# Two tiles of the first normalised rows moved to ScalarE, and rows of x, stores and two additions placed elsewhere in their queues, in a float32 linear-attention block on one core

## The chip, the core and the metric

The kernel runs on one core of a Trainium2 chip. The engines of the core work side by side and meet only at semaphores: TensorE (PE in the profile; PEld is its weight load), VectorE (DVE), ScalarE (ACT), GpSimd (POOL) and SyncE (SP), which here only issues transfers. The metric is the device time of one execution in microseconds, lower is better; the time of a kernel is the median of several executions.

## The reference

```python
x  = hidden_states                      # 4 sequences x 512 tokens x 512, float32
xn = layernorm(x)
qkv = silu(xn @ w_qkv.T)                # 16 heads of 128: q, k, v
for each block of 64 tokens:            # decayed linear attention
    out   = (q * q_decay) @ kv + ((q @ k.T) * diag_decay) @ v
    kv    = block_decay * kv + (k * k_decay).T @ v
out = norm_w * out * rsqrt(mean(out^2) + eps)
s   = (sigmoid(xn @ w_gate.T) * out) @ w_out.T
scores = softmax(xn @ router_w.T + router_bias)        # 64 experts, top 8
f   = xn * sum(top_w) + top_w @ expert_bias[top_idx]
return x + s * silu(f)
```

## The kernel before, in words

Every float32 product is made of three: each operand is split into a part that TensorE takes exactly (`_hi`, rounded by ScalarE) and a rest (`_lo`, the difference, from GpSimd for weights and from VectorE for tokens), and hi x hi, hi x lo and lo x hi are summed in PSUM.

The four sequences are worked in two halves of two sequences (`bp` 0 and 1), each half in eight steps, one for a pair of heads: steps `ss` 0 to 15. A step has four weight groups, QK0, VAL, QK1 and GATE. From step 1 on each group is computed with seven block products (`p1` ... `p7`) over blocks of the transposed tokens, of which four are sums of others (`T1` to `T4`) in Strassen's manner; VectorE's `e1` ... `e7` join the products, and ScalarE applies the activations. Step 0 uses plain products (`direct_block`).

The order on each engine is written out by hand, one function per engine; each engine runs its list from top to bottom, and a wait holds everything behind it.

Opening. SP loads four row tiles of the first sequence (128 tokens x 512 each, into `acc`), the constants, the first weight group (`land_a`), the four tiles of the second sequence, and later the sequences of the second half. VectorE computes statistics of the first four tiles and a Newton step of 1/sqrt (`row_stats`, `row_roots`), then normalises tiles 0, 1 and 2; ScalarE normalises tile 3 (`normalise`, L975), between the two halves of the first weight split (`direct_hi(0, 0)`, `direct_hi(0, 1)`, L1005). GpSimd makes the rests of these weights (`direct_lo`, L1420). PE transposes the tiles strip by strip (`fill(0, 0)` to `fill(0, 3)`, L491; `rows_there` holds the waits on the tiles), ScalarE and VectorE take each result (`take_fill`, L994 and L1634), and `direct_block(0)` begins (L524 to L526).

Transition between the halves. The transposed tokens of the second half wait in device memory. In step 7 SP loads them block by block (`load_block`, L373 and L374; four transfers of 256 KB for each block) into the places that the step's GATE products have left free, in the order B21, T2, T1, T3, T4, B22, after it has issued the load of step 8's VAL weights (L316, 512 KB). In step 8 (`close`) the first half is finished: for each of eight row tiles `sum0` (VectorE, L1824) joins the experts' product with the row of x from `res_buf` (`load_res`, L426), ScalarE applies Silu, `scale0` (L1837) multiplies, `finish0` (GpSimd, L1483) adds the row of x, and `store0` (L430) writes the tile out. The ring `res_row` holds four rows, so `load_res(t + 4)` comes after `finish0(t)`. Rows 4 and 5 are loaded ahead of the load of the next QK0 weights and the turning of the keys (`swap_keys`), rows 6 and 7 behind them. The last two additions, `finish0(6)` and `finish0(7)`, and their stores belong to step 9: on GpSimd they stand ahead of the work on the QK1 weights (`raw_lo`, `weight_sums`, `sums_lo`), on SP ahead of the load of the GATE weights (L323), which waits until `sums_lo` has freed `land_a`.

In every step from 1 on the values are turned through device memory: `values_out` (L354) writes a block of 256 KB, `values_back` (L361) reads two of them back in four transfers of 128 KB made of short packets, once for each sequence, and `kv_products` (L677) on PE waits for them.

Of the kernel before, what the change touches and what calls it, by code (L numbers as in the profile page):

```python
# [15 lines left out]
NCH = SEQ // CH  # L16
# [4 lines left out]
TILES = 2 * NCH  # L21
# [16 lines left out]
def lightning_block(nc: bass.Bass, x, wgrp, wv, wo, consts_d, router_w, expert_b, out):  # L38
# [9 lines left out]
    with ExitStack() as ctx:  # L48
# [262 lines left out]
        def _(sp):  # L311
# [58 lines left out]
            def load_block(blk):  # L370
                at = place(PAIRS, blk)
                for k in range(2):
                    sp.dma_start(xt_hi[:, at, k, :].bitcast(F32), spill_hi[2 * blk + k]).then_inc(block_in[blk], 16)  # L373
                    sp.dma_start(xt_lo[:, at, k, :].bitcast(F32), spill_lo[2 * blk + k]).then_inc(block_in[blk], 16)  # L374

            def step(pair, ss):
                close = ss == PAIRS
                after = (pair + 1) % PAIRS
                if close:
                    sp.wait_ge(top_turned, 2)  # L380
                    for t in range(4):
                        load_res(t)
                swap_keys(ss, 0)
                if ss == PAIRS - 1:

                    sp.wait_ge(router_made, 2)
                    load_block(B11)
                values_out(ss, 0)
                if ss == PAIRS + 1:
                    store0(6)  # L390
                    store0(7)
                load_group(pair, ss, GATE)
                load_out(pair, ss)
                values_out(ss, 1)
                values_out(ss, 2)
                values_back(ss, 0)
                values_out(ss, 3)
                values_back(ss, 1)
                if close:
                    for t in range(2):  # L400
                        store0(t)
                        load_res(t + 4)
                if ss < LAST:
                    load_group(after, ss + 1, QK0)
                swap_keys(ss, 1)
                if ss == LAST:
                    return
                if close:
                    for t in range(2, 4):
                        store0(t)  # L410
                        load_res(t + 4)
                load_group(after, ss + 1, VAL)
                if ss == PAIRS + 1:
                    load_block(B12)
                if ss == PAIRS - 1:
                    for blk, used in ((B21, P2), (T2, P6), (T1, P5), (T3, P7), (T4, P4), (B22, P3)):
                        sp.wait_ge(prod, prods(group(ss, GATE)) + used)
                        load_block(blk)
                if close:
                    store0(4)  # L420
                load_group(after, ss + 1, QK1)
                if close:
                    store0(5)
# [50 lines left out]
        def _(pe):  # L474
# [18 lines left out]

            def rows_there(bp, b, c):

                if bp == 0 and c < 3 - b:
                    pe.wait_ge(ln_row, 3 * b + c + 1)
                elif bp == 0:
                    pe.wait_ge(ln_row_a, c if b else 1)
                elif b == 0:  # L500
                    pe.wait_ge(ln_row, 5 + c + 1)
                else:
                    pe.wait_ge(ln_row_a, 3 + c + 1)

            def direct_block(j, quarters=range(4)):

# [456 lines left out]
        def _(act):  # L963
# [291 lines left out]
            act.wait_ge(eps_set, 2)  # L1255
            act.preload_act_table(ACT.Sqrt)
            root_std(0)
            direct_hi(0, 0)
            normalise(0, 0, 0, 3)
            direct_hi(0, 1)  # L1260
            for f in range(4):
                take_fill(0, f)
            values_hi()
            root_std(1)
# [114 lines left out]
        def _(pool):  # L1379
# [5 lines left out]

            def token_sums0():

                pool.wait_ge(ln_row, 5)
                pool.wait_ge(ln_row_a, 3)
                pool.wait_ge(xt_turned, filled(0, 1))  # L1390
                pool.tensor_tensor(half_rows(0, 0), half_rows(1, 0), half_rows(0, 0), ALU.subtract).then_inc(t_row, 1)
                pool.wait_ge(t_row, 1)
                pool.wait_ge(xt_turned, filled(0, 5))
                pool.tensor_tensor(half_rows(1, 0), half_rows(1, 1), half_rows(1, 0), ALU.subtract).then_inc(t_row, 1)
                pool.wait_ge(t_row, 2)
                pool.wait_ge(xt_turned, filled(0, 7))
                pool.tensor_tensor(half_rows(1, 1), half_rows(1, 1), half_rows(0, 0), ALU.subtract).then_inc(t_row, 1)
                pool.wait_ge(t_row, 3)
                pool.tensor_tensor(half_rows(0, 1), half_rows(0, 1), half_rows(1, 1), ALU.subtract).then_inc(t_row, 1)

            def token_sum1(i):
# [3 lines left out]
                dst = half_rows(*((0, 0), (1, 0), (1, 1), (0, 1))[i])  # L1405
                first, second = ((b12, b11), (b22, b12), (b22, half_rows(0, 0)), (b21, half_rows(1, 1)))[i]
                if i == 0:
                    pool.wait_ge(ln_row, 5 + NCH)
                    pool.wait_ge(ln_row_a, 3 + NCH)
                pool.wait_ge(xt_turned, filled(0, 9 + 2 * i))  # L1410
                pool.wait_ge(t_row, NCH + i)
                pool.tensor_tensor(dst, first, second, ALU.subtract).then_inc(t_row, 1)
# [79 lines left out]
            def step(bp, ss):  # L1492
# [10 lines left out]
                add_square(bp0, before, 1, 0)  # L1503
                sums_lo(ss, VAL)
                add_square(bp0, before, 1, 1)
                if ss == PAIRS + 1:
                    finish0(6)
                    finish0(7)
                raw_lo(ss, QK1)
                weight_sums(ss, QK1)  # L1510
                sums_lo(ss, QK1)
                if ss == LAST:
                    direct_lo(FINAL, 0)
                    direct_lo(FINAL, 1)
# [58 lines left out]
        def _(dve):  # L1573
# [403 lines left out]
            row_stats(0, range(NCH))  # L1977
            row_roots(0)
            dve.wait_ge(ln_stat, LN_DONE[1])
            for c in range(3):  # L1980
                normalise(0, 0, c)
            for f in range(4):
                take_fill(0, f)
# [158 lines left out]
```

## Time and profile before

| | |
|---|---|
| median of 3 runs | 1076.3 us (1075.11 to 1077.16) |
| profiled execution, own time | 1073.37 us |
| profiled execution, span of its instructions | 1071.6 us |
| PE busy | 1047.8 us, 98% of the span |
| PE weight load busy | 894.9 us, 84% |
| VectorE, ScalarE, GpSimd busy | 752.5, 514.8, 634.3 us |
| chain that ended last | PE 88%, DVE 4%, DMA 3%, SP's queue 2%, POOL 2% |

The span is that of one profiled execution; its own time is 1.8 us longer, and the median of the runs lies 2.9 us above that. Busy time of PE is modelled from pipelined matmuls. The chain is followed back from the last instruction to what released each piece of work.

### The profile page before, as it was taken

Reading aid. Unit: us, or ns where it says so; the run is one execution under the profiler, and the core shown is the slowest. Engines: PE = TensorE matmul, PEld = TensorE weight load, DVE = VectorE, ACT = ScalarE, POOL = GpSimd, SP = SyncE. Lnnn points to the kernel's source line nnn. Section 1 sums busy time; section 2 is a strip of 40 time slices with the busy share of each in tenths; the row PEclk is TensorE's granted clock in tenths of the full one; section 3 lists DMA queues with packets and bytes.
Section 4 is the critical chain, followed back from the end, with each engine's and each line's share of the span. In section 5 each row is a group of like instructions: output and inputs, shape, how many; then the busy total and the mean of one; then the engine's idle time right before and its main releaser. Section 6 shows DMA issues by size and latency. Waiting matters only on the chain.

```text
span 1071.6 us, 15997 instructions
## 1 busy us (share of the span) xinstructions
PE 1047.8 (98%) x5626; PEld 894.9 (84%) x5626; DVE 752.5 (70%) x1287; ACT 514.8 (48%) x806; POOL 634.3 (59%) x513
## 2 busy tenths in 40 slices
PE   5999999999999999999999999999999999999997
PEld 5898888888888888888888788888888888888886
DVE  6857667676765768767677776756767766876866
ACT  4845353453536335453554535445453543535345
POOL 3837475565747557474746856657474755747435
PEclk9999999999999999999999999999999999999999
DMA  7173524435252442526856255352525335252442
GB/s 242 65 279 100 130 79 129 108 98 118 54 134 69 128 89 72 136 68 168 271 191 155 96 141 141 103 114 60 143 70 133 90 101 107 59 123 85 130 127 80
DMA packets 259920, 128.12 MB, mean 120 GB/s; under 512 B 223360, under 2 KB 223488, under 8 KB 259840
## 3 DMA queue, kind: packets, MB, share of 16 engines
q1 hardware_dynamic: 259840, 127.09, 43.7%
q8 instruction: 46, 0.75, 0.3%
q14 instruction: 34, 0.28, 0.1%
HBM read 86.95 MB, written 40.11 MB: 119 GB/s over the span
## 4 chain that ended last, share of the span: by engine, by line
PE 88%; DVE 4%; DMA 3%; SPq 2%; POOL 2%; issue 2%; ACT 1%; POOLq 0%; DVEq 0%
PE st_ps L536 17%; PE st_ps L538 16%; PE st_ps L537 16%; PE out_ps L711 5%; PE score_ps L658 5%; PE out_ps L713 5%; PE out_ps L712 5%; PE head_ps L694 5%; PE head_ps L697 4%; PE tk_ps L677 4%; PE st_ps L524 1%; PE st_ps L525 1%; PE st_ps L526 1%; DMA xt_lo<-spill_lo 1%; DMA k_squares<-v_t 1%
## 5 line engine op out<-in xcount | busy, mean ns | idle before, releaser
L536 PE MATMUL st_ps<-xt_hi,w_hi 128*128 128x512 f32 x826 | 336.8, 408 | 2.6 <-DVE gated L1677 1.6
L538 PE MATMUL st_ps<-xt_hi,w_lo 128*128 128x512 f32 x826 | 323.2, 391 | 0.0
L537 PE MATMUL st_ps<-xt_lo,w_hi 128*128 128x512 f32 x826 | 322.1, 390 | 0.0
L1446 POOL TENSOR_TENSOR w_lo<-land_a,w_hi 128x1024 fp32r<-128x1024 f32 x44 | 107.8, 2449 | 130.0 <-ACT w_hi L1040 130.0
L538 PEld LDWEIGHTS st_ps<-xt_hi,w_lo 128*128 128x128 f32 x826 | 155.0, 188 | 34.6
L536 PEld LDWEIGHTS st_ps<-xt_hi,w_hi 128*128 128x128 f32 x826 | 155.6, 188 | 32.1 <-DVE gated L1677 1.8
L537 PEld LDWEIGHTS st_ps<-xt_lo,w_hi 128*128 128x128 f32 x826 | 155.7, 189 | 27.9
L1426 POOL TENSOR_TENSOR w_lo<-land_a,w_hi 128x768 fp32r<-128x768 f32 x44 | 84.2, 1913 | 147.1 <-ACT w_hi L1035 147.1
L711 PE MATMUL out_ps<-wo_hi,gate_hi 128*128 128x512 f32 x240 | 96.2, 401 | 0.8 <-DVE acc L1762 0.6
L1764 DVE TENSOR_TENSOR acc<-acc,out_ps 128x512 f32<-128x512 f32 x104 | 71.2, 685 | 32.2 <-PE out_ps L713 31.0
L713 PE MATMUL out_ps<-wo_hi,gate_lo 128*128 128x512 f32 x240 | 93.7, 391 | 0.0
L712 PE MATMUL out_ps<-wo_lo,gate_hi 128*128 128x512 f32 x240 | 93.5, 390 | 0.0
L1477 POOL TENSOR_TENSOR acc_sq<-acc_sq,square 128x512 f32<-128x512 f32 x60 | 77.1, 1284 | 25.6 <-ACT square L1131 25.6
L694 PE MATMUL head_ps<-probs,v_row 128*128 128x128 f32 x496 | 85.6, 275 | 0.0
L694 PEld LDWEIGHTS head_ps<-probs,v_row 128*128 128x128 f32 x496 | 74.6, 191 | 5.4 <-issue 0.7
L1087 ACT ACTIVATE k_t<-k_t 128x512 f32<-128x512 f32 x30 | 19.0, 632 | 111.0 <-DVE k_t L1683 111.0
L697 PE MATMUL head_ps<-q_t,state 128*128 128x128 f32 x372 | 71.9, 275 | 0.0
L1749 DVE TENSOR_TENSOR gate_lo<-gated,gate_hi 128x512 fp32r<-128x512 f32 x60 | 70.5, 1177 | 0.5
L658 PEld LDWEIGHTS score_ps<-q_t,k_t 128*128 128x128 f32 x512 | 66.5, 191 | 4.6
L1745 DVE SCALAR_TENSOR_TENSOR gated<-gated,head_ps 128x512 f32<-128x512 f32 x62 | 42.5, 685 | 39.5 <-ACT gated L1081 18.6
L658 PE MATMUL score_ps<-q_t,k_t 128*128 128x128 f32 x512 | 67.3, 274 | 0.0
L1035 ACT ACTIVATE w_hi<-land_a 128x768 fp32r<-128x768 f32 x44 | 37.1, 844 | 58.4 <-DMA land_a<-wgrp_dram 45.2
(330 smaller groups left out, 2069.7 us busy)
## 6 DMA issues: line engine op xcount, KB each, us to landing
land_a<-wgrp_dram SPq DMA_DIRECT2D x48, 512.0 KB, 3.7
v_row<-v_squares SPq DMA_DIRECT2D x120, 128.0 KB, 3.2
k_row<-k_squares SPq DMA_DIRECT2D x120, 96.0 KB, 2.9
v_squares<-v_t SPq DMA_DIRECT2D x45, 256.0 KB, 2.6
land_b<-wo_dram SPq DMA_DIRECT2D x16, 512.0 KB, 4.6
land_b<-wgrp_dram SPq DMA_DIRECT2D x14, 512.0 KB, 4.2
k_squares<-state SPq DMA_DIRECT2D x15, 384.0 KB, 2.3
k_squares<-v_t SPq DMA_DIRECT2D x15, 384.0 KB, 4.7
```

The costliest lines, as they stand in the source:

```text
L536: pe.matmul(ps[:, :], w_h2, x_h2, start=first and k == 0, stop=False, skip_group_check=True)
L537: pe.matmul(ps[:, :], w_h2, x_l2, start=False, stop=False, skip_group_check=True)
L538: end = pe.matmul(ps[:, :], w_l2, x_h2, start=False, stop=last and k == 1, skip_group_check=True)
L658: last = pe.matmul(score_ps[:, at], k_t[:, b, at], q_t[:, h, b, at], start=True, stop=True)
L694: last = pe.matmul(ps[:, at], v_row[:, b, h, c, :], probs[:, b, c, :], start=True, stop=c == 0)
L697: last = pe.matmul(ps[:, at], state[:, b, c - 1, :], q_t[:, h, b, at], start=False, stop=True)
L711: pe.matmul(ps[:, :], hi[:, h, at], wo_hi[:, h, :], start=h == 0, stop=False)
L712: pe.matmul(ps[:, :], hi[:, h, at], wo_lo[:, h, :], start=False, stop=False)
L713: last = pe.matmul(ps[:, :], lo[:, h, at], wo_hi[:, h, :], start=False, stop=h == 1)
L1426: pool.tensor_tensor(flat(w_lo[:, n % 2, 0:3, :, :]), flat(landing(ss, g)[:, 0:3, :, :]), flat(w_hi[:, n % 2, 0:3, :, :]).bitcast(F32), AL ...
L1446: pool.tensor_tensor(flat(w_lo[:, n % 2, 3:7, :, :]), flat(landing(ss, g)), flat(w_hi[:, n % 2, 3:7, :, :]).bitcast(F32), ALU.subtract).th ...
L1477: pool.tensor_tensor(cols_b, cols_b, square[:, :], ALU.add).then_inc(sq_added, 1)
```

## The change

On ScalarE tiles 2 and 3 of the first sequence are normalised ahead of both halves of the first weight split, and the first `take_fill` comes between the halves; VectorE normalises only tiles 0 and 1. The counts that others wait for follow. In step 7 block B21 is loaded ahead of step 8's VAL weights. In step 8 tile 2 is stored and row 6 of x loaded with the first group, ahead of the next QK0 weights and the key turning. In step 9 `finish0(6)` and `finish0(7)` stand behind the QK1 weights on GpSimd, and their two stores behind `values_back(ss, 0)` on SP.

```diff
+            def renew_block(blk, used):
+                sp.wait_ge(prod, prods(group(PAIRS - 1, GATE)) + used)
+                load_block(blk)
...
                 values_out(ss, 0)
-                if ss == PAIRS + 1:
-                    store0(6)
-                    store0(7)
                 load_group(pair, ss, GATE)
                 load_out(pair, ss)
                 values_out(ss, 1)
                 values_out(ss, 2)
                 values_back(ss, 0)
+                if ss == PAIRS + 1:
+                    store0(6)
+                    store0(7)
                 values_out(ss, 3)
                 values_back(ss, 1)
                 if close:
-                    for t in range(2):
+                    for t in range(3):
                         store0(t)
                         load_res(t + 4)
...
                 if close:
-                    for t in range(2, 4):
-                        store0(t)
-                        load_res(t + 4)
+                    store0(3)
+                    load_res(7)
+                if ss == PAIRS - 1:
+                    renew_block(B21, P2)
                 load_group(after, ss + 1, VAL)
...
                 if ss == PAIRS - 1:
-                    for blk, used in ((B21, P2), (T2, P6), (T1, P5), (T3, P7), (T4, P4), (B22, P3)):
-                        sp.wait_ge(prod, prods(group(ss, GATE)) + used)
-                        load_block(blk)
+                    renew_block(T2, P6)
+                    renew_block(T1, P5)
+                    renew_block(T3, P7)
+                    renew_block(T4, P4)
+                    renew_block(B22, P3)
...
-                if bp == 0 and c < 3 - b:
-                    pe.wait_ge(ln_row, 3 * b + c + 1)
+                if bp == 0 and c < 2:
+                    pe.wait_ge(ln_row, 2 * b + c + 1)
                 elif bp == 0:
-                    pe.wait_ge(ln_row_a, c if b else 1)
+                    pe.wait_ge(ln_row_a, 2 * b + c - 1)
...
             root_std(0)
+            normalise(0, 0, 0, 2)
+            normalise(0, 0, 0, 3)
             direct_hi(0, 0)
-            normalise(0, 0, 0, 3)
+            take_fill(0, 0)
             direct_hi(0, 1)
-            for f in range(4):
+            for f in range(1, 4):
                 take_fill(0, f)
...
                 add_square(bp0, before, 1, 1)
+                raw_lo(ss, QK1)
+                weight_sums(ss, QK1)
+                sums_lo(ss, QK1)
                 if ss == PAIRS + 1:
                     finish0(6)
                     finish0(7)
-                raw_lo(ss, QK1)
-                weight_sums(ss, QK1)
-                sums_lo(ss, QK1)
...
-            for c in range(3):
+            for c in range(2):
                 normalise(0, 0, c)
```

## Rows read from the trace of the kernel before

**Rows 1.** Waits of PE: line, waited for whom, us in all, times, longest

```profile
PE out_ps L491 <- DVE acc L1623: 11.2, 2, 10.2
PE st_ps L536 <- DVE gated L1677: 1.6, 1, 1.6
...
PE st_ps L536 <- DMA xt_lo<-spill_lo: 0.8, 1, 0.8
```

**Rows 2.** Timeline of PE from 640 to 650 us

```profile
645.33 0.91 PE L677 MATMUL tk_ps<-v_row,k_row 128*128 128x128 f32 x6 [1.13 <-issue]
```

**Rows 3.** Busy us by window: length, PE, PEld, DVE, ACT, POOL, clock, DMA, GB/s

```profile
300.00:500.00 200.00, 200.00 (x1056) 170.58 (x1055) 143.30 (x252) 92.69 (x144) 118.59 (x97) 1.00 0.43 108
520.00:530.00 10.00, 10.00 (x59) 8.72 (x58) 7.96 (x12) 4.67 (x7) 5.96 (x4) 1.00 0.98 368
```

**Rows 4.** Timeline of the opening: start us, length us, engine, line, operation

```profile
9.51 2.47 DVE L1623 TENSOR_SCALAR acc<-acc,mean_var,rstd 128x512 f32<-128x512 f32 x3
9.73 0.63 ACT L1005 ACTIVATE w_hi<-land_a 128x512 fp32r<-128x512 f32 x1 [1.45 <-DMA land_a<-wgrp_dram]
...
10.27 0.80 ACT L975 ACTIVATE acc<-acc,ln_shift,rstd 128x512 f32<-128x512 f32 x1
10.44 2.67 POOL L1420 TENSOR_TENSOR w_lo<-land_a,w_hi 128x512 fp32r<-128x512 f32 x2 [9.57 <-ACT w_hi L1005]
...
12.77 0.60 ACT L994 ACTIVATE xt_hi<-out_ps 128x512 fp32r<-128x512 f32 x1 [1.18 <-PE out_ps L491]
...
15.96 0.69 DVE L1634 TENSOR_TENSOR xt_lo<-head_ps,xt_hi 128x512 fp32r<-128x512 f32 x1 [0.16 <-ACT xt_hi L994]
```

**Rows 5.** Tile acc from 9 to 13 us: durations in ns, smallest, median, largest

```profile
L1623 DVE TENSOR_SCALAR acc<-acc,mean_var,rstd x3: 540/545/1553, 9.5 to 10.4; 128x512 f32<-128x512 f32 x3
```

**Rows 6.** Chain that ended last, opening: start us, us, what

```profile
12.04 0.69 PE out_ps L491 x2
...
15.29 0.43 PE st_ps L524
...
16.10 0.23 PE st_ps L526
```

**Rows 7.** Tile land_b from 515 to 560 us, with its transfers' time to landing

```profile
L316 SPq DMA_DIRECT2D land_b<-wgrp_dram x1: 656/656/656, 518.1 to 518.1; - x1
L1035 ACT ACTIVATE w_hi<-land_b x1: 847/847/847, 527.5 to 527.5; 128x768 fp32r<-128x768 f32 x1
...
DMA to landing us min/median/max: 4.6/4.7/4.8
```

**Rows 8.** Timeline of POOL from 560 to 600 us

```profile
568.13 3.79 POOL L1483 TENSOR_TENSOR acc<-acc,res_row 128x512 f32<-128x512 f32 x3
```

**Rows 9.** Timeline of SP's queue around the seventh row of x

```profile
573.39 0.43 SPq L426 DMA_DIRECT2D res_row<-x_dram  x1
...
586.73 0.43 SPq L426 DMA_DIRECT2D res_row<-x_dram  x1
```

**Rows 10.** Timeline of DVE from 585 to 600 us

```profile
591.35 0.76 DVE L1824 SCALAR_TENSOR_TENSOR v_ps<-res_row,ffn_small,v_ps 128x512 f32<-128x512 f32 x1 [3.25 <-DMA res_row<-x_dram]
...
594.94 2.84 DVE L1749 TENSOR_TENSOR gate_lo<-gated,gate_hi 128x512 fp32r<-128x512 f32 x1
```

**Rows 11.** Timeline of POOL from 600 to 650 us

```profile
613.62 3.00 POOL L1483 TENSOR_TENSOR acc<-acc,res_row 128x512 f32<-128x512 f32 x2
```

**Rows 12.** Timeline of SP's queue in step 9

```profile
625.83 0.34 SPq L323 DMA_DIRECT2D land_a<-wgrp_dram  x1
...
627.18 1.56 SPq L354 DMA_DIRECT2D v_squares<-v_t  x2
633.88 3.03 SPq L361 DMA_DIRECT2D v_row<-v_squares  x4
...
639.78 3.20 SPq L361 DMA_DIRECT2D v_row<-v_squares  x4
```

**Rows 13.** Transfers issued from 636 to 645 us: count, KB each, us to landing

```profile
v_squares<-v_t SPq DMA_DIRECT2D x1, 256.0 KB, 2.8
```

More of the change, by code:

```diff
@@ L494, in rows_there @@
             def rows_there(bp, b, c):
-                if bp == 0 and c < 3 - b:
-                    pe.wait_ge(ln_row, 3 * b + c + 1)
+                if bp == 0 and c < 2:
+                    pe.wait_ge(ln_row, 2 * b + c + 1)
                 elif bp == 0:
-                    pe.wait_ge(ln_row_a, c if b else 1)
+                    pe.wait_ge(ln_row_a, 2 * b + c - 1)
                 elif b == 0:
-                    pe.wait_ge(ln_row, 5 + c + 1)
+                    pe.wait_ge(ln_row, NCH + c + 1)
                 else:
-                    pe.wait_ge(ln_row_a, 3 + c + 1)
+                    pe.wait_ge(ln_row_a, NCH + c + 1)
             def direct_block(j, quarters=range(4)):
@@ L1386, in token_sums0 @@
             def token_sums0():
-                pool.wait_ge(ln_row, 5)
-                pool.wait_ge(ln_row_a, 3)
+                pool.wait_ge(ln_row, NCH)
+                pool.wait_ge(ln_row_a, NCH)
                 pool.wait_ge(xt_turned, filled(0, 1))
@@ L1407, in token_sum1 @@
                 if i == 0:
-                    pool.wait_ge(ln_row, 5 + NCH)
-                    pool.wait_ge(ln_row_a, 3 + NCH)
+                    pool.wait_ge(ln_row, TILES)
+                    pool.wait_ge(ln_row_a, TILES)
                 pool.wait_ge(xt_turned, filled(0, 9 + 2 * i))
```

## The prediction, made blind

> **What bounds the kernel now.** I read five views: the waits of PE, busy time by window, the timeline and chain of the opening, the tile view of `land_b`, and the timelines of each engine around the transition (steps 7 to 9).
>
> The waits of PE come first. They name three places: the opening (11.2 us, of which 10.2 are the first wait and 1.0 a second one for a tile normalised by VectorE), and in the transition 1.6 us for VectorE's joining and 0.8 us for a block of spilled tokens [rows 1]. PE's timeline has a fourth, 1.13 us before `kv_products` of step 9, labelled "issue" [rows 2]. Elsewhere there is next to nothing: in a long window of the steady state PE is busy for all 200 of 200 us [rows 3]. There no edit on another engine can gain anything; only the stretches where PE waits can. The reader should see that the four parts of the change touch just these places. PE's waits are short and in a row, so what one gives back is kept only if the engines that feed PE come forward too.
>
> **The opening.** VectorE's three normalisations begin at 9.51 and take 2.47 us [rows 4]. The tile view shows why: two took 0.54 us, the third 1.55 us [rows 5], and that one ran while GpSimd made weight rests from 10.44 on [rows 4]. PE's third and fourth strip of `fill(0, 0)` start only at 12.04 and take 0.69 us, so to 12.73 [rows 6].
>
> After the change ScalarE starts its two tiles at about 9.5, when VectorE's own begin. At 0.80 us each [rows 4] both are done by 11.1. VectorE's two need 2 x 0.54 = 1.1 us and end at 10.6, and GpSimd can't be in their way, since it waits for `direct_hi(0, 0)`, now 11.1 to 11.75 (0.63 us). PE needs half of the 0.69 us after 11.1, with a tenth or so for the signal: 11.6, where it was 12.73. That is 1.1 us. The three fills behind it come 1.1 us earlier too, and `direct_block(0)` could start at 14.2, not 15.29 [rows 6].
>
> Do the others keep up? ScalarE: `take_fill(0, 0)` 11.75 to 12.35 (0.60 us) instead of from 12.77; `direct_hi(0, 1)` to 13.0; fills 1 and 2 to 14.2, fill 3 after PE's at 14.2, to 14.8. VectorE's rest of fill 3 then ends near 15.6, where it was 15.96 + 0.69 = 16.65 [rows 4]. The weights' first rest, now moved behind, is one of two in 2.67 us: 11.75 + 1.34 = 13.1, still ahead of 14.2. So the delayed weight split costs nothing; its cover is 1.1 us, and beyond that it would cost one for one. VectorE goes on from fill 3 to the second sequence's statistics, so the gain of 1.0 to 1.1 us is handed on along the chain. I take 1.0.
>
> The matmuls of the chain are spaced 0.43 us at 15.29 and 0.23 us from 16.10 [rows 6]: PE's rate at 1.2 and at 2.4 GHz for 512 columns. If the rise comes earlier with PE's work, all 1.0 stays. If it stays at 16.1, then 1.9 us of block products run at the low level instead of 0.8; the additional 1.1 us do half the work, and 0.55 us is lost. Bounds: 0.5 and 1.1. By the Trainium skill, "TensorE: Matmul & The Clock Gate", Part 1, recent activity releases the clock, and at a point that varies from run to run; that allows either case, and by its activity rule the sum would be 1.0, with a rise fixed in time 0.5. Whether the rise moves is not shown by this trace.
>
> **B21 ahead of VAL (step 7).** VAL's load was issued at 518.1 and landed 4.7 us later, at 522.8; ScalarE took it at 527.5, released by PE [rows 7]. Four issues of B21 come before it now, 1.8 us with the gaps between, and 1 MB, 2.8 us at 368 GB/s [rows 3]. The bytes decide: 525.6. Even both added whole, 527.4, just meets ScalarE. So no cost. Nor a gain: the wait that PE has here (0.8 us [rows 1]) is for a block that is issued later, and the bytes ahead of that one are the same. I take 0; bounds 0 and +0.8 (if the stall went away by a luckier order). If VAL came later than 527.5, ScalarE's whole list would be held, with the VectorE joins of the last GATE group behind it.
>
> **Row 6 earlier (step 8).** `finish0` of tiles 0, 1 and 2 starts at 568.13 and takes 3.79 us, to 571.9 [rows 8]. SP issued row 5 at 573.39 and would come to `store0(2)` at 573.8: nothing to wait for, and row 6 is issued at about 574.3 instead of 586.73 [rows 9]. VectorE waited 3.25 us, to 591.35, for that row alone (586.73 + 4.6) [rows 10]; with row 6 landed near 579 the wait is gone, and what is late next is PE's own product. PE saw 1.6 us of it [rows 1]. SP issues two transfers more (about 0.9 us) ahead of the QK0 weights and the key turning, in a gap of its queue. I take 1.5 for PE, since the `e4` that follows still trails PE by some 0.1 us. Lower bound: VectorE is held later by GpSimd, which ran a weight rest while `gate_lo` took 2.84 us [rows 10] and is not moved by this edit. If VectorE falls in with it again, its next joins stay where they were and PE waits for them instead. A third of the gain, 0.5 us, would be left; at worst 0. Upper bound 1.6.
>
> **finish0(6), (7) and their stores (step 9).** The two additions held GpSimd from 613.62 for 3.00 us [rows 11], in front of the QK1 weights. Behind those they delay nobody that I find; the QK1 rests end about 3 us earlier, and with them the GATE load of 625.83 (L323) that waits for them: about 622.8. It and the `wo` load, 1 MB together (2.8 us), then are out of the way when the value blocks are written at 627.18; before, the blocks were queued behind them, and SP could issue the first `values_back` only at 633.88 [rows 12]. Two issues end at 628.74, and a block lands in 2.8 us when nothing is ahead [rows 13]: 631.5 at the latest, 2.4 us earlier. From one `values_back` to the other it was 5.9 us [rows 12]; the stores now lie between, two issues of 0.45 us and 512 KB, 1.4 us at 368 GB/s. 631.5 + 5.9 + 1.4 = 638.8, or 1.0 us before the old 639.78. `kv_products` stood 1.13 us for this second swap [rows 2]. I take 1.0 for PE; upper bound 1.13; lower bound -1.4, if the first swap does not move and the stores only push the second.
>
> **The sum.** 1.0 + 0 + 1.5 + 1.0 = 3.5 us, from 1073.4 of the profiled execution to 1069.9. The runs' median is 2.9 above that execution; taking the same distance, 1076.3 - 3.5 = 1072.8.
>
> **Rivals.**
>
> *The clock rise stays.* For it: nothing in the trace ties it to the work. Against: it came after PE had been busy without a gap from 12.04 on [rows 6], so a PE that starts earlier may have it earlier. The opening gives 0.5: 1073.3. Chance 0.15.
>
> *GpSimd holds VectorE after row 6.* For: the 1.55 us normalisation [rows 5] and the 2.84 us `gate_lo` [rows 10] show how VectorE stands still beside GpSimd. Against: VectorE comes past that place over 1.6 us earlier, before GpSimd's long instruction. Row 6 gives 0.5: 1073.8. Chance 0.12.
>
> *The stores hold the last value swap.* The first swap doesn't move, and the stores push the second by 1.4: 1.0 + 1.5 - 1.4 = 1.1, so 1075.2. Chance 0.10.
>
> *The change does not do what it says.* The stalls are gone, but PE meets the next late engine some us further on and gets nothing from steps 8 and 9: only the opening, or 1075.8. PE's full 200 us window [rows 3] speaks against it for the steady state, the chain of close waits for it in the transition. Chance 0.08.
>
> *Slower.* The same two stores, but written at the rate of the short packets around them: a swap of 512 KB took from 639.78 to 645.33 [rows 2, 12], 5.6 us. If the first swap does not move, the second comes 5.6 us later, and PE's wait grows by that: 1.0 + 1.5 - 5.6 = -3.1, so 1079.4. It decides from the point where the second swap is issued over 2.5 us after 639.8. Against: writes of whole rows don't come in short packets. Chance 0.04.
>
> **How the numbers follow.** The forecast has 0.51. About 0.2%, 2.2 us, is what a measurement of this kernel can tell from no change, so faster means below 1074.1. The forecast and the first two rivals lie below (0.78 together, of which I count 0.06 as falling short, since the second is 0.3 us from the line): 0.72. Same: the third and fourth, and that 0.06: 0.24. Slower: 0.04. The range: at the low end all upper bounds, 1.1 + 0.8 + 1.6 + 1.1 = 4.6, or 1071.7, rounded to 1071.5; at the high end it takes in the third rival, 1075.3.
>
> **What the changed profile would show.** Opening: one strip wait less, PE's chain into `direct_block(0)` near 14.2; both VectorE normalisations at 0.54 us; GpSimd's first weight rest from about 11.8. If the third and fourth strip still start near 12, step one is wrong. The spacing of matmuls tells when the clock rises. Step 7: VAL still landed when ScalarE asks for it, the 0.8 us wait for the spilled block still there. Step 8: no wait for `res_row`, and no 1.6 us wait of PE at L536. Step 9: the first `values_back` over 2 us nearer to its `values_out`, no "issue" wait at L677. The prediction fails if PE's waits in the transition add up to over 2 us again under other names.

## The result, and the profile after

| | before | changed |
|---|---|---|
| median | 1075.92 us (4 runs, 1075.11 to 1077.16) | 1069.46 us (4 runs, 1068.64 to 1070.33) |
| profiled execution, own time / span | 1073.37 / 1071.6 us | 1068.64 / 1066.8 us |

The medians differ by 6.5 us. The ratio is 0.9948, 95% interval 0.9932 to 0.9964, which is 5.6 us, 3.9 to 7.3. The prediction had 3.5 us and 1072.8, and its range began at 1071.5. The direction was right, the size too small by this comparison, and the level outside the range. In a longer comparison, on one chip with more executions, the same code has 1070.3 against 1074.4 and the ratio 0.9966 (0.9952 to 0.9979), which is 3.7 us, 2.3 to 5.2 (e5 below), close to the forecast gain. The two profiled executions differ by 4.7.

PE's waits in the changed kernel (line, waited for whom, us in all, times, longest):

```profile
PE out_ps L499 <- DVE acc L1633: 9.8, 1, 9.8
PE out_ps L499 <- DVE xt_lo L1644: 1.3, 1, 1.3
PE st_ps L544 <- DMA xt_lo<-spill_lo: 1.3, 2, 0.8
PE out_ps L719 <- DVE acc L1772: 0.5, 1, 0.5
```

Of the waits of before [rows 1] the second one for a tile is gone from the first line, the one for `gated` is gone, and the "issue" wait [rows 2] is gone. The wait for the spilled blocks has grown from 0.8 to 1.3 us, in two pieces. PE's timeline has them:

```profile
534.07 0.47 PE L544 MATMUL st_ps<-xt_hi,w_hi 128*128 128x512 f32 x1 [0.44 <-DMA xt_lo<-spill_lo]
...
539.46 0.47 PE L544 MATMUL st_ps<-xt_hi,w_hi 128*128 128x512 f32 x1 [0.81 <-DMA xt_lo<-spill_lo]
```

How the gain builds up can be read from one recurring instruction, VectorE's first copy into `k_t` (twice in a step; L1677 before, L1687 after). Four of them in the changed kernel:

```profile
503.25 0.69 DVE L1687 COPY k_t<-st_ps 128x512 f32<-128x512 f32 x1 [1.15 <-PE st_ps L546]
...
571.96 0.69 DVE L1687 COPY k_t<-st_ps 128x512 f32<-128x512 f32 x1 [0.53 <-PE st_ps L546]
...
605.18 0.69 DVE L1687 COPY k_t<-st_ps 128x512 f32<-128x512 f32 x1 [2.08 <-PE st_ps L546]
...
667.40 0.69 DVE L1687 COPY k_t<-st_ps 128x512 f32<-128x512 f32 x1 [2.08 <-PE st_ps L546]
```

| copy in | before | changed | difference | added since the last |
|---|---|---|---|---|
| step 1 | 94.22 | 92.65 | -1.57 | -1.57 |
| step 7, second | 504.71 | 503.25 | -1.46 | +0.11 |
| step 8, second | 572.73 | 571.96 | -0.77 | +0.69 |
| step 9, first | 608.08 | 605.18 | -2.90 | -2.13 |
| step 10, first | 672.14 | 667.40 | -4.74 | -1.84 |
| step 15, second | 1019.46 | 1014.73 | -4.73 | 0.00 |

All of the change is made in the opening and in steps 8 and 9, and from step 10 on the difference stands still, as PE's full window [rows 3] had it.

**Opening.** Timeline of the changed kernel:

```profile
9.10 1.52 ACT L983 ACTIVATE acc<-acc,ln_shift,rstd 128x512 f32<-128x512 f32 x2 [1.24 <-DVE ln_shift L1627]
9.10 1.00 DVE L1633 TENSOR_SCALAR acc<-acc,mean_var,rstd 128x512 f32<-128x512 f32 x2
...
9.79 1.36 PE L499 MATMUL out_ps<-consts,acc 128*128 128x128 f32 x4 [9.79 <-DVE acc L1633]
...
10.53 0.61 ACT L1013 ACTIVATE w_hi<-land_a 128x512 fp32r<-128x512 f32 x1
...
11.22 2.51 POOL L1430 TENSOR_TENSOR w_lo<-land_a,w_hi 128x512 fp32r<-128x512 f32 x2 [10.36 <-ACT w_hi L1013]
...
14.38 0.69 DVE L1644 TENSOR_TENSOR xt_lo<-head_ps,xt_hi 128x512 fp32r<-128x512 f32 x1 [0.16 <-ACT xt_hi L1002]
```

ScalarE and VectorE start together at 9.10, each with two tiles; PE has all four strips in one run of 1.36 us; GpSimd starts only at 11.22, when VectorE is long done. The answers to [rows 4]: VectorE 1.00 for two instead of 2.47 for three, the rest of fill 3 at 14.38 instead of 15.96. The chain, against [rows 6]:

```profile
11.15 0.85 PE tk_ps L499 x4
...
13.71 0.43 PE st_ps L532
...
14.96 0.23 PE st_ps L532
```

The first block product is at 13.71, not 15.29, and the spacing falls from 0.43 to 0.23 us at 14.96, not 16.10: in these two executions the rise of the clock came 1.1 us earlier. That it went with the work is not shown: e5, the same kernel again, starts its block products 0.1 us before this one, and by PE's timeline its first spacing of 0.23 us comes only at 15.88 (15.94 in before, 14.79 to 15.03 in the changed kernel).

**B21 ahead of VAL.** The tile view of `land_b`, against [rows 7]:

```profile
L316 SPq DMA_DIRECT2D land_b<-wgrp_dram x1: 430/430/430, 518.8 to 518.8; - x1
L1043 ACT ACTIVATE w_hi<-land_b x1: 848/848/848, 526.0 to 526.0; 128x768 fp32r<-128x768 f32 x1
...
DMA to landing us min/median/max: 4.8/5.1/5.5
```

VAL is issued at 518.8 and lands 4.8 to 5.5 us later, by 524.3; ScalarE takes it at 526.0, released by PE. The order cost ScalarE nothing.

**Row 6.** SP's queue and VectorE, against [rows 9, 10]:

```profile
573.39 0.48 SPq L434 DMA_DIRECT2D res_row<-x_dram  x1
...
585.63 0.43 SPq L434 DMA_DIRECT2D res_row<-x_dram  x1
```

```profile
588.22 0.76 DVE L1834 SCALAR_TENSOR_TENSOR v_ps<-res_row,ffn_small,v_ps 128x512 f32<-128x512 f32 x1 [0.87 <-PE v_ps L755]
...
592.00 0.68 DVE L1759 TENSOR_TENSOR gate_lo<-gated,gate_hi 128x512 fp32r<-128x512 f32 x1
```

Row 6 is issued at 573.39 (586.73 before), row 7 at 585.63. VectorE's `sum0(6)` runs at 588.22 and waited 0.87 us for PE's own product, and `gate_lo` takes 0.68 us where it took 2.84.

**Step 9.** SP's queue and PE's value products, against [rows 2, 12]:

```profile
620.03 0.34 SPq L323 DMA_DIRECT2D land_a<-wgrp_dram  x1
...
623.80 1.88 SPq L354 DMA_DIRECT2D v_squares<-v_t  x2
627.46 3.23 SPq L361 DMA_DIRECT2D v_row<-v_squares  x4
630.74 1.15 SPq L438 DMA_DIRECT2D out_dram<-acc  x2
...
634.94 3.20 SPq L361 DMA_DIRECT2D v_row<-v_squares  x4
```

```profile
640.61 0.91 PE L685 MATMUL tk_ps<-v_row,k_row 128*128 128x128 f32 x6
```

The GATE load is issued at 620.03, the first value swap at 627.46, 3.7 us after its blocks were begun at 623.80 (6.7 before), and PE starts the second value products with no wait.

### The profile page after: what moved, and what is told of

Its sections match the earlier page's. It is cut to its first block, busy times and chain, and to the rows that moved or that the text cites. A ratio compares the mean times of both kernels' runs of the same rounds, so it can differ in the third digit from the quotient of the medians.

```text
span 1066.8 us, 15997 instructions
## 1 busy us (share of the span) xinstructions
PE 1047.1 (98%) x5626; PEld 895.0 (84%) x5626; DVE 750.0 (70%) x1286; ACT 515.5 (48%) x807; POOL 634.2 (59%) x513
## 4 chain that ended last, share of the span: by engine, by line
PE 92%; DVE 2%; DMA 1%; issue 1%; POOL 1%; ACT 1%; SPq 0%; POOLq 0%; DVEq 0%
PE st_ps L544 18%; PE st_ps L546 17%; PE st_ps L545 17%; PE score_ps L666 5%; PE out_ps L719 5%; PE out_ps L721 5%; PE out_ps L720 5%; PE head_ps L702 5%; PE tk_ps L685 4%; PE head_ps L705 4%; PE st_ps L532 1%; PE st_ps L534 1%; PE st_ps L533 1%; DMA xt_lo<-spill_lo 1%; POOL acc L1567 1%
## 5 line engine op out<-in xcount | busy, mean ns | idle before, releaser
L1436 POOL TENSOR_TENSOR w_lo<-land_a,w_hi 128x768 fp32r<-128x768 f32 x44 | 83.9, 1906 | 147.9 <-ACT w_hi L1043 147.9
L1759 DVE TENSOR_TENSOR gate_lo<-gated,gate_hi 128x512 fp32r<-128x512 f32 x60 | 66.4, 1109 | 0.5
```

Source lines behind the costliest of these rows:

```text
L1436: pool.tensor_tensor(flat(w_lo[:, n % 2, 0:3, :, :]), flat(landing(ss, g)[:, 0:3, :, :]), flat(w_hi[:, n % 2, 0:3, :, :]).bitcast(F32), AL ...
```

## The experiments

Each kernel is timed against before in five rounds on one chip; a difference in us is the ratio's, with its 95% interval. The runs of before had medians of 1074.72 (35 runs), 1074.42 (23) and 1074.51 (23) in the three comparisons.

**The parts alone.** e1 has only the opening:

```diff
             root_std(0)
+            normalise(0, 0, 0, 2)
+            normalise(0, 0, 0, 3)
             direct_hi(0, 0)
-            normalise(0, 0, 0, 3)
+            take_fill(0, 0)
             direct_hi(0, 1)
```

> The opening part alone. The trace of the changed kernel has step 1 earlier by 1.57 us, of which 0.4 is an earlier landing of the first rows of x. If the edit makes the gain and it is kept through the transition: 1.1 to 1.2 us faster, all seven steps before step 8 earlier by that much. If the wait for the spilled blocks in step 8 is set by the transfers and not by PE, 0.3 to 0.7 us of it is given back there: 0.5 to 0.9 us faster. If the opening holds what the profiled execution of before hides (the runs' median moved by 6.5 us, the profiles only by 4.7): 2.5 us or more.

Measured: 1073.19 us, ratio 0.9983 (0.9973 to 0.9994), 1.8 us faster (0.6 to 2.9). Its profile is 0.88 us ahead of the profile of before in step 1 and 0.84 to 0.90 ahead through step 9: nothing was given back in step 8. From step 10 on it is 1.55 us ahead and more, since PE waited 0.6 us at the value products of step 9 and not 1.1, although nothing there was changed. At its end only 0.2 us of this is left; where it goes is shown in the last part of this section.

e2 has only row 6 and the store of tile 2:

```diff
-                    for t in range(2):
+                    for t in range(3):
                         store0(t)
                         load_res(t + 4)
...
-                    for t in range(2, 4):
-                        store0(t)
-                        load_res(t + 4)
+                    store0(3)
+                    load_res(7)
```

> Row 6 of x and the store of tile 2 earlier in step 8, alone. By the two traces this part gave 2.1 us up to the first product of step 9 and 0.5 more in it: 2.1 to 2.6 us faster. By the prediction's step (the 1.6 us wait of PE alone): 1.5. If the landing of row 6 varies from run to run and is what makes the runs of before longer than their profile: 3.5 to 4.5 us faster.

Measured: 1072.54 us, ratio 0.9982 (0.9970 to 0.9994), 1.9 us faster (0.6 to 3.2). That lies between the 2.1 to 2.6 expected from the traces and the 1.5 of the prediction's step, and the interval holds both. The profile: 2.1 us between the second copy of step 8 and the first of step 9, as in the changed kernel. PE's wait at the value products of step 9 is smaller than in before too:

```profile
PE tk_ps L676 <- issue: 0.5, 1, 0.5
```

This is not an effect of row 6. In the profiles of other kernels without the whole step 9 edit, none of which moves row 6, this wait is 1.1 us (before), 0.6 (e1), 1.4 (e4), 0.9 (e7), 0.8 (e9) and 0.5 (e10).

e3 has only step 9, both the additions and the stores:

```diff
+                raw_lo(ss, QK1)
+                weight_sums(ss, QK1)
+                sums_lo(ss, QK1)
                 if ss == PAIRS + 1:
                     finish0(6)
                     finish0(7)
...
                 values_back(ss, 0)
+                if ss == PAIRS + 1:
+                    store0(6)
+                    store0(7)
                 values_out(ss, 3)
```

> The two additions and the two stores later in step 9, alone. By the two traces: the wait at the value products is gone and 1.4 us come back, so 1.1 to 1.4 faster. If the stores only push the second value swap: 0.5 slower to 0.5 faster.

Measured: 1074.17 us, ratio 0.9992 (0.9981 to 1.0004), 0.9 us faster (0.4 slower to 2.0 faster). In the profile the "issue" wait is gone and, against the profile of before, 1.45 us come back between the first copies of steps 9 and 10. The runs' interval holds both that and nothing. The wait that the edit takes away is 0.5 to 1.4 us in the kernels just named, 0.8 on average with e2; with the edit it is 0 to 0.4 (0.4 in e5, 0.2 in e6, none in the changed kernel, e3, e11 and e12). From these waits an estimate is 0.7 us, half of what the pair of profiles shows.

e4 has only B21 ahead of VAL:

```diff
+                if ss == PAIRS - 1:
+                    renew_block(B21, P2)
                 load_group(after, ss + 1, VAL)
```

> Block B21 ahead of the VAL weights in step 7, alone. If the 0.7 us that the changed kernel gives back in step 8 comes from this order: 0.5 to 0.8 us slower, with two waits of PE for spilled blocks instead of one. If it comes from PE being earlier in front of a load set by the transfers (as the prediction has this part at nothing): no change within 0.2 us and one wait of 0.8 us.

Measured: 1075.21 us, ratio 0.9996 (0.9984 to 1.0009): no change that can be told. One wait of 0.9 us for a spilled block in the profile.

**The whole, and the whole without B21.** e5 is the changed kernel again; e6 leaves the order of B21 and VAL as before.

> The changed kernel once more, with more executions. If the parts add up (1.8, 1.9 and 0.9 us faster as measured alone, B21 nothing): 4.6 us below before, 1070 us. If they help each other: 6 us and more below. The first normalisation to step 1 takes 83.5 to 83.8 us in the profile, as in the two traces with the new opening, and the spread of the runs is smaller than that of before, because VectorE is no longer caught by GpSimd in the opening.

> The changed kernel with the order of B21 and the VAL weights left as before. If the order is innocent (PE is early in front of a load set by the transfers): the same as the changed kernel within 0.3 us, with 0.4 to 1.3 us of waits for spilled blocks. If the order cost 0.7 us: 0.7 us faster than the changed kernel and one wait.

Measured: e5 1070.32 us, ratio 0.9966 (0.9952 to 0.9979), 3.7 us faster (2.3 to 5.2); its eight runs lie within 1.8 us, those of before within 7.4. e6 1069.33 us, ratio 0.9952 (0.9935 to 0.9970), 5.2 us faster (3.2 to 7.0). The parts alone sum to 1.8 + 1.9 + 0.9 + 0.4 = 5.0, between the two. Between the second copy of step 7 and the second of step 8, where the waits for spilled blocks lie, the profiles with B21 first stand at +0.69 (changed), +0.24 (e4), +0.03 (e5) and -0.23 (e11) against before, the nine others at -0.43 to +0.42. The order does not stand out of what one execution differs from another. e6's median is 1.0 us below e5's, more than the 0.3 expected of an innocent order, but its ratio's interval overlaps e5's, and e12 and e11 below differ by 0.4 only; whether the order costs a few tenths is left open.

**What the opening's edit removes.** The profile of before showed the third tile at 1.55 us. The next kernels with the old opening showed something else. The tile view and the timeline of e3:

```profile
L1623 DVE TENSOR_SCALAR acc<-acc,mean_var,rstd x3: 534/1481/1648, 9.5 to 12.4; 128x512 f32<-128x512 f32 x3
```

```profile
9.45 3.51 DVE L1623 TENSOR_SCALAR acc<-acc,mean_var,rstd 128x512 f32<-128x512 f32 x3
9.55 2.67 POOL L1420 TENSOR_TENSOR w_lo<-land_a,w_hi 128x512 fp32r<-128x512 f32 x2 [8.69 <-ACT w_hi L1005]
...
12.56 1.15 PE L491 MATMUL out_ps<-consts,acc 128*128 128x128 f32 x3 [0.87 <-DVE acc L1623]
```

Two of three tiles take 1.5 us or more, not one. Here GpSimd's first subtraction began at 9.55, a tenth behind VectorE's first tile; in the profile of before it began at 10.44. e7 holds GpSimd back and changes nothing else:

```diff
+            pool.wait_ge(ln_row, 3)
             direct_lo(0, 0)
             direct_lo(0, 1)
```

> Before, with one wait added: GpSimd's first weight rest waits for VectorE's third normalisation; ScalarE still does one tile. Theory: what the opening's edit removed is VectorE standing still during GpSimd's first subtraction (1.55 us for the third tile in the profile of before) or during both (2.4 us in the three other traces with the old opening), so that before is slower by 1 or by 2 us from run to run. Then the three take 1.6 us in all in the profile, step 1 comes 84.0 to 84.4 us after the first normalisation where it was 84.7 to 86.0, and the kernel is 1.2 to 1.6 us faster than before. Rival: the gain is that PE gets the third tile from an engine that is free at once; then holding GpSimd back only delays the weights: 0 to 0.5 us slower.

Its tile view:

```profile
L1624 DVE TENSOR_SCALAR acc<-acc,mean_var,rstd x3: 541/543/547, 9.3 to 10.2; 128x512 f32<-128x512 f32 x3
```

All three tiles are free. Measured: 1073.26 us, ratio 0.9991 (0.9978 to 1.0004), 1.0 us faster (0.4 slower to 2.4 faster). The profile is as the theory had it: 1.46 us for the three, and step 1 comes 83.7 us after the first tile. The runs gained less than the 1.2 to 1.6 expected, and their interval also holds the rival's small loss, so the tiles decide here and not the runs. e10 moves the weights' landing the other way:

```diff
-            sp.dma_start(consts[:, 0:610], consts_d).then_inc(const_in, 16)
             sp.dma_start(land_a[:, :, :, :].rearrange("p a k o -> p (a k o)"), wgrp[0]).then_inc(w_in, 16)
+            sp.dma_start(consts[:, 0:610], consts_d).then_inc(const_in, 16)
```

> Before, with the first weights (512 KB) loaded ahead of the constants (305 KB). Theory: how much VectorE loses in the opening hangs on when the weights land, since that starts GpSimd; landing about 0.8 us earlier, GpSimd catches two or three of VectorE's three tiles in every execution: the three take 3.4 us or more in the profile (1.5 where none was caught), step 1 comes 85.6 us or more after the first normalisation, and the kernel is 0.3 to 1.5 us slower than before. Rival: earlier weights help, since the first product can start sooner: 0.3 us faster or nothing.

Measured: 1073.94 us, ratio 0.9994 (0.9985 to 1.0003), 0.6 us faster (0.3 slower to 1.6 faster): a miss. The profile has two tiles caught and 3.36 us, but the weights were taken at 8.74, hardly earlier than in e3 (8.84) or e4 (8.86) and later than in e2 (8.26), so the dose was not changed, and two caught tiles are what four of the seven profiles with this opening and GpSimd free have. The openings of all profiles side by side, from their timelines (us from the start):

| kernel | first VectorE tile | GpSimd starts | VectorE's tiles take | tiles caught | first tile to step 1's copy |
|---|---|---|---|---|---|
| e3, old | 9.45 | 9.55 | 3.51 (3) | 2 | 86.0 |
| e10, old | 9.08 | 9.45 | 3.36 (3) | 2 | 85.8 |
| e4, old | 9.46 | 9.57 | 3.36 (3) | 2 | 85.7 |
| e2, old | 8.61 | 8.97 | 3.36 (3) | 2 | 85.7 |
| e9, old | 9.20 | 9.97 | 2.41 (3) | 1 | 84.7 |
| before, old | 9.51 | 10.44 | 2.47 (3) | 1 | 84.7 |
| e8, old | 8.93 | 10.09 | 1.46 (3) | 0 | 83.9 |
| e7, old, GpSimd held | 9.26 | 10.80 | 1.46 (3) | 0 | 83.7 |
| changed, e1, e5, e6 | 9.00 to 9.62 | 11.1 to 11.7 | 1.00 (2) | 0 | 83.6 to 83.7 |

One tile caught costs 1 us, two cost 2. Two are caught where GpSimd starts 0.10 to 0.37 us behind VectorE, one at 0.77 and 0.93, none at 1.16 and more; and what GpSimd waits for is the weights' landing and ScalarE's first split behind it [rows 4]. The table and e7 show that GpSimd's start decides; that the landing sets it is read from the waits, since e10 did not move it. With none caught the old opening is within 0.1 to 0.3 us of the new one.

**Which half of the step 9 edit.** e8 moves the stores alone, e9 the additions alone.

> Before, with the two stores of step 9 behind the first value swap on SP, and GpSimd's two additions left in front of the QK1 weights. The prediction's third rival alone: the first swap does not move and the stores push the second, so PE's wait at the value products grows from 1.1 to 2.5 us: 1.4 us slower than before. If the stores are hidden beside the short packets of the first swap: no change, or up to 0.5 us faster since the GATE load is issued at once.

> Before, with GpSimd's two additions of step 9 behind the QK1 weights, and the two stores left where SP meets them ahead of the GATE load. The QK1 rests end 3 us earlier, but SP stands at the stores until the additions are done, about 625 us, so the GATE load is issued when it was: no change, or up to 0.5 us slower, since the stores' bytes now lie right in front of the loads, and the wait at the value products stays at 1 us or grows. If the additions alone were the cause of that wait: 1.1 us faster and no wait.

Measured: e8 1077.57 us, ratio 1.0039 (1.0023 to 1.0054), 4.2 us slower (2.5 to 5.8), three times what was expected. e9 1073.71 us, ratio 0.9999 (0.9988 to 1.0010), no change. SP's queue in e8, windows of e8 (columns as in [rows 3]) and PE's timeline:

```profile
623.38 1.56 SPq L354 DMA_DIRECT2D v_squares<-v_t  x2
630.04 3.39 SPq L361 DMA_DIRECT2D v_row<-v_squares  x4
633.48 1.15 SPq L430 DMA_DIRECT2D out_dram<-acc  x2
634.67 0.45 SPq L354 DMA_DIRECT2D v_squares<-v_t  x1
637.69 3.23 SPq L361 DMA_DIRECT2D v_row<-v_squares  x4
```

```profile
630.00:640.00 10.00, 9.68 (x47) 7.84 (x46) 5.53 (x10) 2.18 (x5) 3.48 (x4) 1.00 0.63 144
640.00:650.00 10.00, 6.31 (x21) 4.96 (x20) 3.03 (x7) 3.59 (x6) 3.68 (x3) 0.66 0.68 156
650.00:660.00 10.00, 10.00 (x60) 8.70 (x59) 4.76 (x8) 3.80 (x7) 8.09 (x7) 1.00 0.54 173
```

```profile
644.46 1.62 PE L677 MATMUL tk_ps<-v_row,k_row 128*128 128x128 f32 x6 [3.69 <-issue]
645.73 0.77 PE L536 MATMUL st_ps<-xt_hi,w_hi 128*128 128x512 f32 x1
...
649.29 0.63 PE L538 MATMUL st_ps<-xt_hi,w_lo 128*128 128x512 f32 x1
...
650.23 0.40 PE L538 MATMUL st_ps<-xt_hi,w_lo 128*128 128x512 f32 x1
```

The first swap is issued 6.7 us behind its blocks, as before; the stores follow it, and the second swap comes 7.65 us after the first, 1.75 more than the 5.9 of before. From its issue to PE's products it also takes 6.77 us, where before takes 5.55. PE waits 3.69 us. That is 2.6 more than before, though a part of it is PE's own lead: it came to this place at 640.77, 3.4 us earlier than before (644.20). More is lost by the clock: after this wait the matmuls are spaced 0.43 us from 645.73 to 649.3 and 0.24 us again at 650.23, and the granted clock of the window is 0.66. By the difference to before in PE's timeline, -0.87 us at 644.46 against 645.33 and +1.66 six microseconds on, this costs another 2.5 us. Together that is 5.1 us in this profile, within the interval of the runs' 4.2. In e9 the stores hold SP in front of the GATE load:

```profile
624.09 1.58 SPq L430 DMA_DIRECT2D out_dram<-acc  x2
625.72 0.43 SPq L323 DMA_DIRECT2D land_a<-wgrp_dram  x1
```

The GATE load goes out at 625.72, as before (625.83), whatever GpSimd does for the QK1 weights. So neither half gains. Both together gain in the profile (e3), by 0.9 us in the runs, whose interval holds nothing too.

**A version that goes on.** With the transition cleared, PE's longest wait behind the first is 0.9 to 1.4 us for the rest of fill 8. e11 takes it up on the changed kernel, e12 the same without the B21 part.

```diff
             dve.wait_ge(ln_stat, LN_DONE[3])
+            take_fill(0, 8)
+            take_fill(0, 9)
             for c in range(NCH):
                 normalise(1, 0, c)
-            for f in range(8, 12):
+            for f in range(10, 12):
                 take_fill(0, f)
```

> The changed kernel, with VectorE's rests of fills 8 and 9 ahead of its four normalisations of the third sequence. PE waited 0.9 to 1.4 us there for the rest of fill 8. It then waits instead for the normalised rows, which come 1.2 us later than now but are asked for 0.9 us after: 0.3 to 0.8 us faster than the changed kernel. If another engine holds PE at the same place: nothing.

> As e11_fills, with B21 and the VAL weights in the order of before. If the order of B21 costs 0.3 to 0.7 us as two profiles hint: 1.0 us below e5_all's version. If it is chance from one execution to the next: the same as e11_fills.

Measured: e11 1069.48 us, ratio 0.9953 (0.9941 to 0.9965), 5.1 us faster than before (3.8 to 6.3); e12 1069.10 us, ratio 0.9948 (0.9936 to 0.9960), 5.6 us (4.3 to 6.9). Against e5's 1070.32 that is 0.8 and 1.2 us, in different comparisons. The wait is gone from e11:

```profile
PE out_ps L499 <- DVE acc L1633: 9.8, 1, 9.8
PE out_ps L719 <- DVE acc L1772: 0.6, 1, 0.6
```

and step 1's copy comes 83.0 us after the first tile instead of 83.6. e12 has the lowest median of all kernels here, within the noise of e11.

**What differs between executions of any kernel.** In four of the fourteen profiles (before, changed, e9, e10) PE keeps its full rate to the end. In the other ten the rate falls, shortly after or within a row of one-column products (L740, L742; the sums of squares) at 1042 to 1054 us. PE has no listed wait there. Windows of before and of e3:

```profile
1050.00:1060.00 10.00, 10.00 (x54) 8.61 (x54) 6.95 (x15) 8.52 (x15) 6.05 (x5) 1.00 0.08 29
1050.00:1060.00 10.00, 10.00 (x47) 8.49 (x48) 5.36 (x13) 6.99 (x12) 4.59 (x4) 0.83 0.01 2
```

In e3 the products of 512 columns are then spaced 0.43 us from 1052.4 to 1055. From the first one-column product to the first of `v_ps<-wo_hi` PE takes 11.3 us in the four, 12.9 in e1, e2, e3, e4, e5, e7 and e11, and 14.5 in e6, e8 and e12, so 1.6 or 3.2 us are lost, with old and new code alike. The runs agree in kind: of the 81 executions of before in the three comparisons, the 25 with a mean granted clock of 0.998 or more have a median of 1073.4 us, the other 56 one of 1075.5.

e10's profile has one more such fall, in step 8, behind the wait that the edit of row 6 removes:

```profile
593.57 0.60 PE L536 MATMUL st_ps<-xt_hi,w_hi 128*128 128x512 f32 x1 [1.82 <-DVE gated L1677]
590.00:600.00 10.00, 8.18 (x43) 6.97 (x42) 7.76 (x10) 3.78 (x6) 7.59 (x8) 0.83 0.53 167
```

It loses 1.4 us there against before, beside the wait. e3 (1.84 us) and e9 (1.78) waited as long at the same place and kept the rate.

## Why the prediction was right in direction and wrong in size

**The opening, taken as 1.0.** The mechanism was right: VectorE's tile was held by GpSimd, and step 1 comes 1.16 us sooner after the first tile (83.55 for 84.71), so none of the covers was used up. This term of the sum was mis-sized. I read the price of the collision from one execution, in which one tile was caught (1.55 us, [rows 5]), and bounded the gain at 1.1 above. In five of the seven profiles with the old opening and GpSimd free another number of tiles was caught, in four of them two, and there the edit is worth 2.1 to 2.4 us (85.7 to 86.0 against 83.6). e1's runs gained 1.8. The rows had the sign of it: GpSimd was released only when the weights had landed, 1.45 us after ScalarE was ready [rows 4], so the price hung on a transfer. The Trainium skill, "SBUF — State Buffer", section "SBUF: two separate sides", says of the shared ports that whichever of a two-port VectorE instruction and a GpSimd instruction "starts first gets the pair for the whole instruction; the other fully blocks". The traces agree with the blocking: each caught tile took 1.48 to 1.65 us instead of 0.54, and none was only slowed a little. On the order they agree only to about a tenth of a microsecond: by the recorded starts e3's first tile began 0.10 us ahead of GpSimd and took 1.65 us, e4's began 0.11 ahead and took 0.54. Weighed before the run, the sentence would have said that the order of two starts decides, which varies.

**The clock rise stays: not settled, and small.** In the changed profile it moved from 16.10 to 14.96, by 1.14 of the 1.58 us by which the first block product moved. The block products of before ran 0.8 us at the low level, those of the changed kernel 1.25; half of the 0.44 us more is 0.2 us lost, not 0.5. In e5, the same kernel, the rise came at 15.88 by PE's timeline, nearly where before has it there (15.94), and step 1 came 0.2 us later after the first tile (83.74 for 83.55). So the rise varies between executions of one kernel, and its price in the opening was some 0.2 us either way.

**B21, taken as 0.** Right for VAL's landing (524.3 at the latest; I had 525.6), and the runs show no change (e4). That the wait for spilled blocks stays was right in kind; it was 1.3 us in this execution, 0.6 to 1.3 in the four profiles with B21 first, and 0 to 1.0 in the profiles with the order of before.

**Row 6, taken as 1.5.** The mechanism was right, to the issue time (574.3 forecast in before's time; 573.39 in a kernel that is 0.8 us ahead there). The term was too small: the traces give 2.1 us up to the first copy of step 9. PE lost 1.6 us at the wait itself, 0.1 at the next start, and 0.25 at `p6` of step 9, where VectorE's joining, late since `gate_lo`, held it for less than a wait that is listed; the rest is in starts of about 0.1 us. I had taken the listed wait as the whole loss. The wait is no constant either: in the profiles with the old step 8 it is 0.6 us (e8) to 1.8 (e3, e9, e10), and in e10 the fall of the clock behind it took another 1.4. The rival in which GpSimd holds VectorE again fell: `gate_lo` took 0.68.

**Step 9, taken as 1.0.** Right in mechanism and nearly in size: the GATE load goes out 5.80 us earlier, 2.45 more than the first group of value blocks just ahead of it had moved (617.07 against 620.42), and the swap is 3.0 us closer to its blocks (2.4 forecast), 1.4 us back in e3's profile, and 0.9 in its runs. The profile of before had a long wait at this place, so what the edit is worth in most executions is nearer the 0.7 us estimated above. The rival of the stores was real: e8 is that rival by itself. Its price, 1.4 us, was too small by two thirds: the swap itself took 1.2 us longer, and PE lost its clock behind the wait, which I had left out of every price.

**The step that failed by most** is the last of the sum: "taking the same distance". It added to the forecast of the profiled execution the 2.9 us by which before's profiled execution was below its runs' median. The changed kernel's was only 0.8 us below its own. This distance is no property of the kernel. The profiled execution of before had one tile caught where four of seven have two, which is 1 us, and it kept PE's full rate to the end, where ten of fourteen lose 1.6 or 3.2 us; the changed kernel's profile kept it too. The other part is that the median of three runs, 1076.3, was high; with 23 to 35 runs it is 1074.4 to 1074.7. Why the first runs lay at 1075.1 to 1077.2 is open: chance in these same two places would do it, but these executions have no trace. Forecast from 1074.5, the same 3.5 us give 1071.0; the kernel has 1069.5 to 1070.3. So 0.7 to 1.5 us are left after the level. The traces put them in the opening (1.0 taken, 2.1 to 2.4 in the executions with two tiles caught) and in row 6 (1.5 taken, 2.1 in the traces), less 0.3 by estimate in step 9. By e5's comparison alone (3.7 us, 2.3 to 5.2) no error in the size can be told from the noise. The two intervals of the whole (3.9 to 7.3 and 2.3 to 5.2) overlap, and the runs don't narrow the gain further.

**Two slips in the working.** The fourth rival, "only the opening", is 1076.3 - 1.0 = 1075.3 by its own terms, not 1075.8; no chance hangs on it. And PE's waits named a further place that the prediction passed over as next to nothing, 1.4 us up to 39.54 us, for the rest of fill 8. No part of the change touches it, so it left the sum as it was; e11 is the kernel that takes it up.

## What to carry to other kernels

A collision whose start hangs on a transfer has no single price: look at what released the second engine, and if it is a landing, take the price of both orders and not that of the profiled execution. The same holds for the level: compare the granted clock, window by window, before adding one execution's distance from the median to a forecast. A wait listed on the bounding engine is less than the loss it stands for, since late joins and many starts of 0.1 us follow it; the distance between two recurring instructions shows the whole. When additions on one engine gate stores on a queue, and both stand in front of a load, look at them as one edit: here neither helped when moved alone.

## What the runs showed of the hardware

After one wait of 3.69 us in full work PE's granted clock fell to 0.66 in a window of 10 us (1.00 in the windows before and after), the matmuls of 512 columns were spaced 0.43 instead of 0.23 us for about 4 us, and 2.5 us were lost beside the wait itself (e8). After a wait of 1.82 us it fell to 0.83 in e10, and 1.4 us were lost; after waits of 1.84 us (e3) and 1.78 us (e9) at the same place it did not fall. The Trainium skill, "TensorE: Matmul & The Clock Gate", section "HAM oscillation — how this bites in real kernels", says that idle gaps make the array start cold again; the row of e8 agrees. At the end of the kernel the clock fell in ten of fourteen profiles at a row of one-column products, with no listed wait of PE ahead of it, and 1.6 or 3.2 us were lost; there the measurement stands without such a gap.

VectorE gets between two GpSimd subtractions that follow each other, and GpSimd between two tiles of VectorE: with both queued the tiles took 1.65, 1.48 and 0.53 us in this order beside two subtractions of 1.27 and 1.36 (e3), so each caught tile waits for about one GpSimd instruction and not for both.
